# Another order of score tiles, key tiles, splits and masks in the cross-attention of a fused decoder layer

## The reference

```python
q = rmsnorm(x @ Wq.T -> (4, 32 heads, 256, 128), q_norm_w)
k = rmsnorm(ctx @ Wk.T -> (4, 8 heads, 1601, 128), k_norm_w)
v = ctx @ Wv.T -> (4, 8 heads, 1601, 128)
scores = q @ k.T / sqrt(128) + mask        # each key head serves 4 query heads
out = softmax(scores) @ v
x = layernorm(x + out @ Wo.T)
```

## Time and profile before

| what | value |
|---|---|
| median of 3 runs | 2526.08 us (2525.43 to 2528.13) |
| the profiled execution | 2523.99 us |
| its span | 2522.2 us |
| mean granted TensorE clock | 0.994 |
| PE busy, whole span | 2389.3 us (95%) |
| DVE, ACT, POOL busy | 73%, 64%, 55% |
| PE, DVE, ACT, POOL busy in 1200 to 2200 us | 932, 752, 739, 651 us |
| DMA share there | 0.78 |

### The profile page before, as it was taken

One profiled execution on the slowest core, in us unless ns is written; L12 is line 12 of the kernel. 1 busy time (PEld: TensorE's weight loads), 2 busy tenths in 40 slices (PEclk: granted clock), 3 DMA queues, 4 the chain that ended last, 5 costly groups with the idle time before them and its releaser, 6 DMA issues.

```text
span 2522.2 us, 44822 instructions
## 1 busy us (share of the span) xinstructions
PE 2389.3 (95%) x12414; PEld 1644.2 (65%) x12414; DVE 1846.0 (73%) x2769; ACT 1612.7 (64%) x3248; POOL 1399.5 (55%) x1239
## 2 busy tenths in 40 slices
PE   9999999999999996999999999999999999998999
PEld 8878888888888874555555555555555555555887
DVE  5899999995774354777777777777777777775544
ACT  3178777786634555777777777777777777775321
POOL 0177777877511346666666666666666666653000
PEclk9999999999999998999999999999999999999999
DMA  6343334434453464877777777777777778777532
GB/s 229 111 128 105 112 117 125 125 105 129 157 184 111 146 203 110 177 188 174 185 175 186 171 187 175 185 175 186 170 186 171 188 176 184 173 159 210 160 110 67
DMA packets 740851, 398.29 MB, mean 158 GB/s; under 512 B 485072, under 2 KB 687952, under 8 KB 740784
## 3 DMA queue, kind: packets, MB, share of 16 engines
q1 hardware_dynamic: 740784, 397.49, 61.3%
HBM read 183.85 MB, written 96.11 MB: 111 GB/s over the span
## 4 chain that ended last, share of the span: by engine, by line
PE 65%; DVE 10%; issue 9%; DMA 7%; ACT 4%; SPq 3%; POOL 2%; DVEq 1%; ACTq 0%; POOLq 0%
PE banks L206 17%; PE banks L207 17%; PE banks L208 17%; PE banks L1137 8%; DMA pT_dma<-halves 6%; PE banks L2568 3%; DVE pT_lo L2501 3%; DVE p_odd L2464 2%; DVE p_even L2464 2%; PE banks L436 2%; ACT pT_hi L2423 1%; SPq L2181 1%; ACT k_hi L2381 1%; DVE halves L2286 1%; SPq L2130 1%
## 5 line engine op out<-in xcount | busy, mean ns | idle before, releaser
L1058 DVE TENSOR_SCALAR_CACHE_REDUCE flags<-abs_s,thr 128x1376 bf16<-128x1376 f32 x256 | 403.7, 1643 | 1.1
L206 PE MATMUL banks<-k_hi,q_hi 128*128 128x416 f16 (+1 forms) x1024 | 341.5, 333 | 11.5 <-DVE t_min L2464 9.1
L2464 DVE CUSTOM_DVE_ANT_0 p_even<-banks,minus_mask,guard_scalars 128x1664 f32<-128x1664 f32 x128 | 249.7, 1951 | 128.5 <-PE banks L208 127.1
L2464 DVE CUSTOM_DVE_ANT_0 p_odd<-banks,minus_mask,guard_scalars 128x1664 f32<-128x1664 f32 x128 | 249.7, 1951 | 128.5 <-PE banks L208 126.7
L207 PE MATMUL banks<-k_lo,q_hi 128*128 128x416 f16 (+1 forms) x1024 | 341.1, 333 | 0.0
L208 PE MATMUL banks<-k_hi,q_lo 128*128 128x416 f16 (+1 forms) x1024 | 340.9, 333 | 0.0
L2423 ACT CAST pT_hi<-banks 128x512 f16<-128x512 f32 x384 | 217.4, 585 | 185.1 <-PE banks L2568 184.0
L2501 DVE TENSOR_TENSOR pT_lo<-banks,pT_hi 128x512 f16<-128x512 f32 (+1 forms) x384 | 258.3, 687 | 45.9 <-ACT pT_hi L2423 45.9
L2396 ACT ACTIVATE p_even<-p_even,t_min 128x1601 f32<-128x1601 f32 x128 | 209.0, 1633 | 69.8 <-DVE t_min L2468 69.0
L2396 ACT ACTIVATE p_odd<-p_odd,t_min 128x1601 f32<-128x1601 f32 x128 | 208.9, 1632 | 52.9 <-DVE t_min L2468 52.1
L206 PE MATMUL banks<-pT_hi,v_hi 128*128 128x512 f16 x320 | 123.0, 384 | 91.6 <-DVE pT_lo L2501 89.1
(11 more groups left out here) (283 smaller groups left out, 6453.5 us busy)
## 6 DMA issues: line engine op xcount, KB each, us to landing
raw<-keys SPq DMA_DIRECT2D x32, 800.5 KB, 4.9
keys<-kT_sb SPq DMA_DIRECT2D x50, 512.0 KB, 4.7
values<-v_sb SPq DMA_DIRECT2D x50, 512.0 KB, 3.0
raw<-values SPq DMA_DIRECT2D x32, 768.0 KB
queries<-qT_sb SPq DMA_DIRECT2D x64, 256.0 KB, 2.6
raw<-queries SPq DMA_DIRECT2D x32, 512.0 KB, 5.3
r_sb<-query_roots SPq DMA_DIRECT2D x32, 512.0 KB, 6.7
inv_b<-inverse_sums SPq DMA_DIRECT2D x64, 256.0 KB, 3.4
```

The source lines that it names most:

```text
L206: pe.matmul(out, a_hi, b_hi, start=start, stop=False)
L1058: bits.done(dve.tensor_scalar(flags[:, tt % 2], abs_s[:, tt], thr[:, tt:tt + 1].bitcast(F32), 0.0, ALU.is_lt, ALU.add, accum_out=out[:, tt ...
L2464: dve.tensor_tensor_reduce(banked(p_sb[u % 2][:, j, 0:KP]), psum[:, 0:SB, 0:SW], banked(minus_mask[:, j % 2]), guards.score_scale, 3.40282 ...
```

## The change

The three tables change, and with them the places at which the other engines do their part. A P tile is used at places 0, 1, 2, 5, 8, 11; scores stand at 0, 3, 6, 9; tiles 3, 4, 5 are turned behind places 2, 5, 8. In `sync` the inverse is stored at place 4 and no longer at 0, behind the loads, which move from 4 to 3. In `vector` the inverse is taken at place 3, and the lo halves stand ahead of `split_p`. In `scalar` exps stand at 2, 5, 8 behind `split_p`, and the hi parts of keys (place 0) ahead of those of queries (place 3). `split_tail` moves from DVE's place 12 to POOL's place 11 and becomes four operations of 128 x 128 for two. In the first unit both mask rows are prepared on POOL, the first three transposes are issued inside `queries`, and halves and value tail are made sooner.

```diff
-    P_AT = (0, 1, 2, 3, 7, 10)
+    P_AT = (0, 1, 2, 5, 8, 11)
-    AT = {0: 1, 4: 2, 7: 3, 10: 0}
-    TURN_AT = {0: 3, 4: 4, 7: 5, 10: 0, 11: 1, 12: 2}
+    AT = {0: 1, 3: 2, 6: 3, 9: 0}
+    TURN_AT = {2: 3, 5: 4, 8: 5, 10: 0, 11: 1, 12: 2}
...
+            if last_trip(i) and s - TT in (4, 5, 7):
+                attention.early["turn_halves"](sp, 0, 0, (4, 5, 7).index(s - TT))
...
-    def split_tail(dve, item, slot):
+    def split_tail(pool, item, slot):
...
-            dve.scalar_tensor_tensor(at, at, low, raw, ALU.mult, ALU.add).then_inc(v_lo_done, 1)
+            pool.tensor_scalar(at, at, low, 1.0, ALU.mult, ALU.mult).then_inc(v_lo_done, 1)
+        for n, (x, raw, _) in enumerate(TAILS):
...
+            pool.tensor_tensor(at, at, raw, ALU.add).then_inc(v_lo_done, 1)
...
         if s == -2:
...
-            pool.tensor_scalar(minus_mask[:, 1, 0:KV], minus_mask[:, 1, 0:KV], -7e34, guards.mask_scale, ALU.max, ALU.mult
+            for r in range(S // P):
...
+                pool.tensor_scalar(minus_mask[:, r, 0:KV], minus_mask[:, r, 0:KV], -7e34, guards.mask_scale, ALU.max,
...
         if s == 6:
...
             repeat_tail(pool, 0, 0, 3)
+            halves_lo_pool(pool, 0, 0, 3)
+            split_tail(pool, 0, 0)
...
-            if pos == 6 and after:
+            if pos == 5 and after:
                 halves_hi_pool(pool, i, u + 1, 2)
...
+            if pos == 11 and splits_v(i, u):
+                split_tail(pool, *v_item(i, u))
...
-        halves_lo_pool(pool, 0, 0, 3)
         for n in range(len(KQ)):
             split_kq_lo(pool, 1, 1, n)
...
+        if s == 6:
+            halves_hi_act(act, 0, 0, 3)
...
-            if pos in (0, 4, 7) and after:
-                exp(act, i, *scored(u, pos))
+            if pos in (2, 5, 8) and after:
+                exp(act, i, u + 1, TURN_AT[pos] - 2)
...
-            if pos in (0, 7) and after:
-                halves_hi_act(act, i, u + 1, AT[pos])
+            if pos in (2, 8) and after:
+                halves_hi_act(act, i, u + 1, TURN_AT[pos] - 2)
...
-            dve.tensor_scalar(minus_mask[:, 0, 0:KV], minus_mask[:, 0, 0:KV], -7e34, guards.mask_scale, ALU.max, ALU.mult
...
-            if pos == 0:
-                invert(i, u)
...
+            if pos == 3:
+                invert(i, u)
+            if pos in (0, 6) and after:
+                halves_lo_dve(dve, i, u + 1, 0 if pos == 0 else 2)
...
-            if pos in (0, 7) and after:
-                halves_lo_dve(dve, i, u + 1, 0 if pos == 0 else 2)
```

More of the change, by code:

```diff
@@ L2108, in columns @@
         return slice(0, P), slice(a, b)
-    KQ = [split(q_raw, q_hi, q_lo, columns(0, 2 * QW)), keys(slice(0, SB // 2)), keys(slice(SB // 2, SB))]
+    KQ = [keys(slice(0, SB // 2)), keys(slice(SB // 2, SB)), split(q_raw, q_hi, q_lo, columns(0, 2 * QW))]
     V = [split(v_raw, v_hi, v_lo, columns(0, NT * HD // 2)), split(v_raw, v_hi, v_lo, columns(NT * HD // 2, NT * HD))]
@@ L2203, in position @@
             after = exists(i, u + 1)
-            if pos == 0:
-                store_inverse(i, u)
-            if pos == 3 and after:
+            if pos == 2 and after:
                 turn_halves(sp, i, u + 1, 0)
-            if pos == 4 and not last_trip(i):
+            if pos == 3 and not last_trip(i):
                 if u % 2:
@@ L2231, in position @@
                 store_o(i, u)
[L2233 to L2236, removed]
+        turn_halves(sp, 0, 0, QT - 1)
+        load_next_v(sp, 1)
         rows.store(sp, G // 2 - 1, 1)
@@ L2257, in scale_v @@
             pool.tensor_scalar(x, x, guards.v_scale, 1.0, ALU.mult, ALU.mult).then_inc(v_scaled, 1)
-    def split_tail(dve, item, slot):
-        wait_apart(dve, v_hi_done, done(len(V) * (item + 1) - 1), dve_passed)
-        for x, raw, low in ((v_hi, v_raw[:, TAIL:], low_rows[:, 0:1]), (v_lo, tail_raw, low_rows[:, 1:2])):
+    TAILS = ((v_hi, v_raw[:, TAIL:], low_rows[:, 0:1]), (v_lo, tail_raw, low_rows[:, 1:2]))
+    def split_tail(pool, item, slot):
+        wait_apart(pool, v_hi_done, done(len(V) * (item + 1) - 1), pool_passed)
+        for x, _, low in TAILS:
             at = x[slot][:, TAIL:]
-            dve.scalar_tensor_tensor(at, at, low, raw, ALU.mult, ALU.add).then_inc(v_lo_done, 1)
+            pool.tensor_scalar(at, at, low, 1.0, ALU.mult, ALU.mult).then_inc(v_lo_done, 1)
+        for n, (x, raw, _) in enumerate(TAILS):
+            at = x[slot][:, TAIL:]
+            pool.wait_ge(v_lo_done, done(V_PARTS * item + len(V_BODY) + n))
+            pool.tensor_tensor(at, at, raw, ALU.add).then_inc(v_lo_done, 1)
     def repeat_tail(pool, i, u, j):
@@ L2328, in early_gpsimd @@
             repeat_tail(pool, 0, 0, 0)
-        if s in (4, 5):
-            split_body_lo(pool, 0, 0, s - 4)
-        if s == 6:
[L2332 to L2336, removed]
+            scale(pool, 1)
+        if s == 3:
+            halves_lo_pool(pool, 0, 0, 1)
+            repeat_tail(pool, 0, 0, 1)
+            split_body_lo(pool, 0, 0, 0)
+        if s == 4:
+            halves_hi_pool(pool, 0, 0, 2)
+            repeat_tail(pool, 0, 0, 2)
+            split_body_lo(pool, 0, 0, 1)
+        if s == 6:
             repeat_tail(pool, 0, 0, 3)
+            halves_lo_pool(pool, 0, 0, 3)
+            split_tail(pool, 0, 0)
     def gpsimd(pool):
@@ L2351, in position @@
                 repeat_tail(pool, i, u + 1, 1)
[L2352 to L2355, removed]
-            if pos == 6 and after:
+            if pos == 5 and after:
                 halves_hi_pool(pool, i, u + 1, 2)
                 repeat_tail(pool, i, u + 1, 2)
-            if pos == 7 and splits_kq(i, u):
+            if pos == 6 and splits_kq(i, u):
+                split_kq_lo(pool, *kq_item(i, u), 2)
                 split_kq_lo(pool, *kq_item(i, u), 1)
-            if pos == 7 and splits_v(i, u):
+            if pos == 6 and splits_v(i, u):
+                split_body_lo(pool, *v_item(i, u), 0)
                 split_body_lo(pool, *v_item(i, u), 1)
@@ L2378, in split_kq_hi @@
         raw, hi, _ = KQ[n]
-        act.wait_ge(*((k_in, landed(item)) if n else (scaled, done(item))))
+        act.wait_ge(*((k_in, landed(item)) if n < 2 else (scaled, done(item))))
         act.wait_ge(s_done, done(QT * 2 * (item - 1) - 1))
@@ L2487, in early_vector @@
             dve.wait_ge(pads, 7)
+        if s == 4:
+            halves_lo_dve(dve, 0, 0, 0)
         if 1 < s <= 5:
@@ L2623, in attention @@
     return Stage(sync, gpsimd, scalar, vector, tensor, {
[L2624 removed]
+        "open": open_counts, "rows": rows, "turn_halves": turn_halves, "first_loads": first_loads, "first_v": lambda sp: load_v(sp, 0), "last_v": last_v,
         "second_kq": lambda sp: load_next_kq(sp, 1), "last_exp": lambda act: exp(act, 0, 0, QT - 1), "gpsimd": early_gpsimd,
```

43 lines of the change are left out of this document (16 added, 27 removed).

## The result

| | before | the change |
|---|---|---|
| median | 2525.76 us (4 runs) | 2507.56 us (4 runs, 2504.08 to 2510.17) |
| profiled execution, span | 2523.99, 2522.2 us | 2510.17, 2508.3 us |
| first and last `take_o` | 1013.3 and 2317.5 us | 1005.3 and 2303.3 us |
| one unit, mean | 20.70 us | 20.60 us |

What follows compares the result with a forecast made beforehand. PE's own work and its waits bound a unit. From 2523.99, 13 for the first unit and 61 x 1.03 came off, 1 was added: 2449, and 2.1 for the median gave 2451 us; range 2435 to 2488.

Steps and rivals of the forecast that it cites:

- Part 1: PE's wait at place 3 for DVE's lo part of P tile 3: all 1.46 us a unit gained.
- Part 3: PE's turn of tile 0 waits 0.69 us for ACT's last exp, costing 0.43 us a unit.
- Part 2: Scores closer together: masks just in time in gaps of 2.39 us, DVE's 4.01 fits in 4.43; cost nothing.
- part 5: Value tail moved from DVE to POOL: 1.9 us of POOL's time, within some 2.2 to spare; cost nothing.
- Part 4: Inverse stored behind the loads: lands at 16 us into the unit, leaving `take_o` 0.8 us of slack; nothing lost.
- the first rival: Inverse's store lands at 17.9 us, `take_o` 1.1 late in 31 units: 34 us given back, 2485; chance 0.18.
- The slower rival: Inverse's read-back queued on SP, store landing from 19.3 us on: 78 us lost, at 20.0 99, 2550; chance 0.04.
- Part 6: First unit, masks on POOL and transposes issued inside `queries`: 13 us gained, bounds 8 and 18.
- the third rival: Wait returns at place 3 for D tiles, transposes landing 1.2 us later: about 2510; chance 0.06.

Runs made afterwards that it cites:

- e2: The changed kernel with ACT making the two copies for P tile 5 behind the fourth exp, not ahead of it; 2487.47 us (0.9860).
- e1: The changed kernel with POOL's work at places 1 and 6 held until DVE's lo half there is done; 2455.01 us (0.9732).
- e5: The changed kernel with POOL held behind DVE's lo half at place 1 alone; 2457.28 us (0.9738).
- e3: The changed kernel with SP storing the inverse ahead of the loads of place 3, not behind them; 2646.58 us (1.0482).
- e8: e7 with the inverse made at place 9 of the unit before, stored and read back by SP at place 0; 2592.90 us (1.0269).
- e9: e7 with the inverse made at place 9 of the unit before, stored at place 0, read back at place 6; 2483.25 us (0.9843).
- e7: The changed kernel with the edits of e1, e2 and e4 together; 2422.99 us (0.9608).
- e10: e7 with the value tail's two operations on DVE again; 2439.86 us (0.9671).
- e4: The changed kernel with one of the two mask rows prepared on DVE again; 2499.58 us (0.9905).

## Why the prediction was wrong

- **Part 1 was right.** The 1.46 us at place 3 are gone.
- **Part 3 was right.** The turn of tile 0 stands 0.70 us (0.69 forecast), and e2 takes it away.
- **Part 2 is the step that failed**: "needs 2.83 + 1.18 = 4.01 at most". The 1.18 came from a unit in which POOL's work had all but ended when the lo half began. The change puts the half right behind the mask and ahead of the split, so it begins while POOL's operation at place 1 has 1.0 to 1.8 us to go, and it takes 1.96 or 2.54 us at place 0. From mask to mask that makes 4.71 and 5.26 us where 4.43 were free: 0.27 and 0.77 us at the score in alternate units, 0.52 on the mean, 32 us in 61 units. e1 and e5 show it: with the two kept apart nothing of it is left. No rival named it, though the earlier trace rows had such a meeting, the 1.20 us for 0.36 of part 5. The Trainium skill (GPSIMD Engine Reference, Key points) says that GpSimd shares its SBUF interfaces with VectorE and contends with VectorE instructions that have two SBUF inputs. The traces agree: the lo half has two (1.09 us alone, up to 2.78 in the change), masks and splits have one and keep their times. I applied it to the value tail, whose operations POOL runs in 0.37 and 0.43 us there, and not to the lo half.
- **Part 4: the first rival came in part, and its slack was mis-sized.** SP waits for the store's landing in the units with a load of keys:

```profile
SPq L104 <- DMA inverse_sums<-p_invT: 27.1, 25, 1.4
```

The read-back goes out 17.7 us into the unit where 16 was taken, and `take_o` starts at 21.6. Of these 1.7 us 1.0 is the load, which goes out at 8.7 and not 7.7 by the slowed half. The rest is the store: the read-back follows the load by 9.0 us in e1 as in the change, where 8.3 had been taken. So the 0.8 us of slack was not there: in e1 `take_o` starts at 20.6, just in time. The change loses 0.4 us on the median in each second unit, some 13 us and not the rival's 34, and e1 has none of it. The slower rival's place was right too: e3, e8 and e9 lose 60 us and more against the kernels that they start from, where the load goes out 1.8 to 4.2 us later; for e3 and e8 a part of that is the clock.
- **Part 5**: 1.6 us for the tail (1.9 taken), at no cost that the waits show, as forecast. That it "delayed no one" on DVE does not hold at e7's pace, where e10 puts the move at 17 us; at the change's own pace it was not tried.
- **Part 6**: 8 of 13 us, its lower bound, and for the reasons named there: both masks on POOL start the first subtraction late (1.3 us by e4), and the value tail stands ahead of the list (1.5). The other 2 us are not accounted for.
- **Luck.** 2507.56 us lies within 3 of the third rival's 2510, but by another way: from 1200 to 2200 us PE has no wait for a landing in the change.

The sum with part 2 and 4 as measured: 18.96 of PE's work, 0.70, 0.52, some 0.2 for the output and 0.1 of small gaps are 20.5 us a unit, against 20.60 measured. That a half costs 0.9 us more in one unit (1.96) and 1.5 in the next (2.54) follows from how much of POOL's operation is left when it begins. The traces show this taking of turns and not what enforces it.

## What to carry to other kernels

A duration read from a trace holds for the neighbours that it had there: before an operation is moved, list what runs on the other engines at its new time, DVE's operations with two inputs in SBUF against POOL's above all, and ask which of the two will have begun first. Where an interval must hold a fixed chain between two matmul groups, ask which of its members can stretch. A large load sets when everything queued behind it lands, so a wait put ahead of the load moves all of that, while a small transfer that is needed soon must not stand right behind it.

## Not expected of the hardware

- A DVE subtraction of 128 x 896 with two SBUF inputs took 1.09 us alone. When it began while POOL worked, it took what was left of POOL's operation and 0.95 us more, within 0.01 us in each of the 97 cases in the change, whether POOL's operation had one input (scaling 128 x 1664) or two.
- POOL's operation that had begun first kept its time (1.65 us for that scaling), and its next one stood 0.83 to 0.85 us longer: 2.62 for 1.77 us in the key split, 1.20 for 0.37 in the scaling of 128 x 128. So the one that looks slow need not be the one that was there first.
- Transposes behind 1.8 MB of loads landed 9.7 to 10.1 us (medians of seven kernels) after the load's issue whether they were issued 1.9 or 4.1 us behind it.
